# Gated delta-rule scan on one core: the query product of two time steps in one GpSimd instruction

## The reference, cut to what matters

```
def step(state, inp):
    q_t, k_t, v_t, a_t, b_t = inp
    state = a_t[..., None, None] * state
    stored = jnp.einsum('bhij,bhj->bhi', state, k_t)
    delta = b_t[..., None] * (v_t - stored)
    state = state + jnp.einsum('bhi,bhj->bhij', delta, k_t)
    o_t = jnp.einsum('bhij,bhj->bhi', state, q_t)
    return (state, o_t)
_, outs = jax.lax.scan(step, state0, (qT, kT, vT, aT, bT))
```

## Time and profile before

| | us |
|---|---|
| median of 3 runs | 2835.84 |
| lowest, highest | 2834.82, 2837.74 |
| the profiled execution, its own time | 2834.44 |
| its span, first to last instruction | 2832.7 |
| mean granted TensorE clock | 0.788 of full speed |

### The profile page before, as it was taken

The page is one execution under the profiler, slowest core; times in us unless marked ns, Lnnn a source line. Parts: engine busy times, 40 slices in busy tenths (PEclk is TensorE's granted clock), DMA queues, the critical chain, the costliest instruction groups (busy, mean ns, idle before and its releaser), DMA issues. The chain is left out here.

```text
span 2832.7 us, 58672 instructions
## 1 busy us (share of the span) xinstructions
PE 1812.1 (64%) x15340; PEld 1408.9 (50%) x15341; DVE 1967.8 (69%) x5192; ACT 1416.0 (50%) x3723; POOL 1404.3 (50%) x1495
## 2 busy tenths in 40 slices
PE   3666665756454566666338888888886546666661
PEld 2443544435352344545217777777775524454551
DVE  5898888989478544444658888888885694544446
ACT  4666666666322334333217777777776223333331
POOL 2544544445300466666306666666666006666661
PEclk8787776767655788888759999999998557888896
DMA  0000000000240111111521111111111401111116
GB/s 24 12 16 19 23 12 23 13 21 19 72 113 6 32 44 42 43 42 43 151 65 32 34 33 32 35 31 33 33 33 35 105 0 42 43 43 43 43 43 191
DMA packets 184180, 121.31 MB, mean 43 GB/s; under 512 B 23288, under 2 KB 172704, under 8 KB 183968
## 3 DMA queue, kind: packets, MB, share of 16 engines
q1 hardware_dynamic: 146560, 68.36, 9.3%
q0 software_dynamic: 18432, 37.79, 5.0%
q10 hardware_dynamic: 18976, 12.59, 1.5%
HBM read 65.70 MB, written 44.04 MB: 39 GB/s over the span
## 5 line engine op out<-in xcount | busy, mean ns | idle before, releaser
L1735 POOL TENSOR_TENSOR att_pl<-att_p,att_ph 128x384 f16<-128x384 f32 x512 | 461.4, 913 | 280.8 <-ACT att_ph L1951 274.2
L1000 POOL DMA_INDIRECT ffn_xs<-normed,ffn_tokeni x288 | 293.3, 1019 | 415.2 <-DVE ffn_empty L1364 147.8
L324 POOL TENSOR_TENSOR sq<-states,qS 128x256 f32<-128x256 f32 x256 | 241.4, 943 | 355.0 <-DVE states L725 328.2
L537 ACT ACTIVATE decayed<-states,alpha 128x64 f32<-128x64 f32 x1024 | 272.3, 336 | 242.7 <-DVE states L725 241.9
L1006 POOL DMA_INDIRECT picked<-ffn_ys,ffn_targeti x288 | 293.4, 1019 | 185.9 <-DVE ffn_ys L1389 120.9
L1195 ACT ACTIVATE ffn_h<-bank,b_cols 128x256 f32<-128x256 f32 x576 | 234.6, 472 | 277.2 <-PE bank L1097 134.6
L2033 DVE TENSOR_REDUCE att_mx<-bank 128x3 f32<-128x384 f32 x512 | 282.6, 553 | 93.2 <-PE bank L1792 93.2
L1097 PE MATMUL bank<-ffn_xh,w_h 128*128 128x256 f16 x576 | 180.1, 313 | 224.0 <-DVE ffn_xl L1371 144.5
L1948 ACT ACTIVATE att_p<-bank 128x384 f32<-128x384 f32 x512 | 252.4, 493 | 122.2 <-PE bank L1825 115.9
L380 PE MATMUL bank<-sq,ident 128*128 128x128 f32 x1024 | 250.0, 415 | 94.7 <-POOL sq L324 94.7
L380 PEld LDWEIGHTS bank<-sq,ident 128*128 128x128 f32 x1024 | 224.6, 252 | 129.9 <-POOL sq L324 101.7
(11 more groups left out here) (336 smaller groups left out, 5343.0 us busy)
## 6 DMA issues: line engine op xcount, KB each, us to landing
ffn_yg<-picked SPq DMA_DIRECT2D x64, 256.0 KB, 4.7
ffn_x_all<-x SPq DMA_DIRECT2D x16, 512.0 KB, 7.2
normed<-ffn_xn ACTq DMA_DIRECT2D x32, 256.0 KB, 2.3
att_qz<-att_qp SPq DMA_DIRECT2D x256, 32.0 KB, 1.9
ffn_xs<-normed,ffn_tokeni POOLq DMA_INDIRECT x288
picked<-ffn_ys,ffn_targeti POOLq DMA_INDIRECT x288
xin<-in_x SPq DMA_DIRECT2D x64, 64.0 KB, 1.9
xres<-in_x SPq DMA_DIRECT2D x64, 64.0 KB, 2.0
```

What stands on the lines that cost most here:

```text
L324: nc.gpsimd.tensor_tensor(sq[:, t, :].rearrange("p (h i j) -> p h i j", h=HL, i=D), states[:, t, :].rearrange("p (h i j) -> p h i j", h=HL ...
L537: ins = nc.scalar.activation(decayed[:, 64 * h:64 * h + 64], states[:, (t - 1) % TC, 64 * h:64 * h + 64], ACT.Copy, scale=alpha[p][:, t, h ...
L1000: pool.indirect_dma_start(xs[j % AHEAD][:, r, :], None, A["normed"], bass.IndirectOffsetOnAxis(ap=tokeni[:, BR * j + r:BR * j + r + 1], ax ...
L1735: nc.gpsimd.tensor_tensor(pl[:, h % RP, :], p32[:, h % RP, :], ph[:, h % RP, :], ALU.subtract).then_inc(low_done, 1)
```

## The change

POOL issues the product only in odd steps, for that step and the one before it together: 2 x 256 values, with the same waits put together (`state_ready` of the odd step, and at the first pair of a chunk or quarter what the even step waited for), and counts `sq_ready` by two. The side work of POOL keeps its steps; in an even step it now stands behind no product of that step. Nothing else is changed.

```
                 for t in range(TC):
-                    pool.wait_ge(state_ready, c * TC + t + 1)
-                    if t == 0:
-                        pool.wait_ge(prep_dve, prep_at(PREP, c, "q_scan"))
-                    if t % (TC // OQ) == 0 and behind(i, p):
-                        pool.wait_ge(o_sums, OQ * (c - 1) + t // (TC // OQ) + 1)
-                    qb = qS[p][:, 32 * t:32 * t + 32].rearrange("p (h j) -> p h j", h=HL).unsqueeze(2)
-                    nc.gpsimd.tensor_tensor(
-                        sq[:, t, :].rearrange("p (h i j) -> p h i j", h=HL, i=D),
-                        states[:, t, :].rearrange("p (h i j) -> p h i j", h=HL, i=D),
-                        qb.to_broadcast([P, HL, D, D]), ALU.mult).then_inc(sq_ready, 1)
+                    if t % 2 == 1:
+                        a = t - 1
+                        pool.wait_ge(state_ready, c * TC + t + 1)
+                        if a == 0:
+                            pool.wait_ge(prep_dve, prep_at(PREP, c, "q_scan"))
+                        if a % (TC // OQ) == 0 and behind(i, p):
+                            pool.wait_ge(o_sums, OQ * (c - 1) + a // (TC // OQ) + 1)
+                        qb = qS[p][:, 32 * a:32 * a + 64].rearrange("p (th j) -> p th j", j=D).unsqueeze(2)
+                        nc.gpsimd.tensor_tensor(
+                            sq[:, a:a + 2, :].rearrange("p t (h i j) -> p (t h) i j", h=HL, i=D),
+                            states[:, a:a + 2, :].rearrange("p t (h i j) -> p (t h) i j", h=HL, i=D),
+                            qb.to_broadcast([P, 2 * HL, D, D]), ALU.mult).then_inc(sq_ready, 2)
                     if behind(i, p):
```

## The result

| | before | changed |
|---|---|---|
| median, us | 2835.33 (4 runs) | 2861.94 (4 runs) |
| lowest to highest | 2833.94 to 2837.74 | 2854.98 to 2864.99 |
| profiled execution, span | 2832.7 | 2859.8 |

The medians differ by 26.6 us; the ratio is 1.0089 (95% interval 1.007 to 1.0109): slower. The forecast was 2860 in 2843 to 2876.

What follows compares the result with a forecast made beforehand. DVE bounds the scan (busy 614 of 691 us) and POOL idles behind it; 17.9 over 14 chunks, 2.4 at chunk starts, 1.1 in chunk 0, 3.4 in chunk 15 and 0.5 at the end give +25.3, 2860, range 2843 to 2876.

Steps and rivals of the forecast that it cites:

- the gap beneath `delta`: Window of 0.52 us from the end of `prod` to `outer`; a 256-value product just fits, one of 512 doesn't.
- The length of the pair: The 512-value product takes 1.26 us alone, 1.50 beside `prod`, ending 1.55 after `prod`'s start; bounds 1.07 and 1.44.
- Rivals 2 and 3: Rival 2: pair quicker, 1.07, total 2847, chance 0.12. Rival 3: no POOL time saved, pair 1.44, total 2873, chance 0.14.
- step 6: DVE waits 2.1 us for PE there, which covers the pair: 0; the wait at `ab_scan` about unchanged.
- step 12: `log1p` waits for the pair, `beta_v` goes next and `outer` ends later: +0.47 us per chunk.
- steps 10 and 15: Step 10: `h13` and `outer` held, +0.53, `og` ahead of `h11`, +1.01. Step 15: `kabS` before `prod`, -0.88 and +0.78.
- Rival 1: DVE keeps the way while its operations overlap, so steps 10 to 12 get shorter: -6 us, 2828, chance 0.12.
- step 4: 0.7 us of transpose or PSUM work behind `prod` hides the pair: 0.
- Chunk 0: First chunk of the scan, without `ounit` and `og`: about +1.1 us.
- Chunk starts: Pair holds `prod` 0.54 longer, covered by `stats`' wait for the load; `gE` reaches into `outer`: +0.27, 9 times.
- step 2: No side work there; `outer` waits for the pair and ends at 1.84 instead of 1.37: +0.47 us per chunk.

Runs made afterwards that it cites:

- e2: Changed kernel with the even step's product of each pair left out, so half the products are missing: 2709.0 against 2705.97 for the kernel before, ratio 1.0006.
- e3: Kernel before, with only the products of steps 2 and 3 of a chunk made one 512-value operation, beside step 4: 2698.23 against 2705.97, ratio 0.997.
- e1: Changed kernel with POOL also waiting for the state of steps 10 and 14 before their side work: 2713.76 against 2705.97 for the kernel before, ratio 1.0027.

## Why the prediction was right

- *POOL's shorter products give nothing directly.* Right: POOL is busy 57 us less and nothing is faster for it.
- *A POOL operation and a two-input DVE operation exclude each other; the gap beneath `delta` holds 256 values and not 512.* Right, and shown from both sides: half the length at the same place loses nothing (`e2`), the full length beneath a transpose loses nothing (`e3`), and costs 0.47 in the same step of chunk 0, which has no transpose. (`xn`, one tensor and two values per partition, is held too, as the earlier trace rows show.)
- *The length of the pair, 1.26, and 1.55 from `prod`.* The end is 1.55 after `prod` in each of the steps shown. The duration beside `prod`, forecast as 1.50, goes from 1.28 to 1.54 with the moment of issue, 0.27 to 0.01 behind `prod`. Rivals 2 and 3, a quicker and a dearer pair, fall with it. (Rival 2's terms add up to about +0.4 a chunk and not +0.6; nothing hangs on it.) The last pair of the scan, alone:

```profile
754.44 1.26 POOL L326 TENSOR_TENSOR sq<-states,qS 128x512 f32<-128x512 f32 x1 [2.75 <-DVE states L727]
```

- *Steps.* But for step 6 none is off by more than 0.07 us; the largest, step 12, was set too high. The rule that went into steps 10 and 15, that the one issued first goes first, decided +1.01 and held there; `e1` shows the size of it by taking it away. Rival 1, DVE keeping the way wherever its operations overlap, is refuted by step 10: `og`, issued 0.13 before `h11`, goes before it though `outer` still runs. But the observation that the rival started from is there too, in step 4 (last section), so neither rule covers all rows.
- *Chunk 0.* +1.1 forecast, +0.8 measured, and partly luck: the forecast left out step 4, which cost 0.47 there, and step 6 came out 0.64 shorter.
- *Chunk starts.* The sum was near (0.35 for 0.27) and the path to it wrong: I had POOL go first as before, but DVE did, by 0.01 us; the wait for the load then swallowed what `prod` gained. Nor are the nine alike: `prod` waited 0.5 in seven of them before, and `stats` for the load in eight. That the mean came out near is luck.
- *Step 6 as cover.* Right for the pair, but the wait isn't "about unchanged": its row went from 32.0 to 27.9. On the means the steps 6 give back about 2 us, and by so much the scan came out better than the sum. That term I had at zero.
- *Total.* 25.3 forecast for the whole. The median moved by 26.6, of which 23.0 are in the scan and 3.6 outside it, where I had none. The two misses partly cancel, so that the total is nearer than its parts is luck.

The Trainium skill's rule of an exclusive lock ("SBUF — State Buffer", "SBUF: two separate sides") agrees in kind: the later one waits, and the earlier one isn't slowed. Its "for the whole instruction" is a little more than the rows show: in the step 2 above `outer` ends 0.27 behind the pair and not its own 0.42, so up to 0.15 us of the two lie side by side.

## What to carry to other kernels

Fewer and longer operations on an idle engine are no gain by themselves when they and the operations of the engine that bounds the kernel hold each other up: look first at what the bounding engine does in each of its gaps, and give the other an operation that fits the gap. Where a product is taken out of a queue, whatever stood behind it moves up; a wait that pins it to its old place cost nothing here and was worth 19 us. Placed by the gaps, the same work made the kernel 35 us faster, and 45 with the earlier load.

## What the runs showed of the hardware that was not expected

Who goes first is decided by hundredths of a us: at chunk starts `prod` 0.05 behind POOL's product waited 0.5 us, and `prod` 0.01 ahead of the pair made POOL wait instead.

The order of issue isn't the whole rule. In step 4 the product is issued 0.10 before `prod` in the kernel before, the pair 0.03 before it in the changed kernel and in `e3`, and `prod` goes first each time, in all 15 chunks that have an `xn`. In step 10 of the changed kernel `og` is issued 0.13 before `h11` and goes first, in all 14. In both a DVE operation was still running; it was `xn` in the one and `outer`, which POOL had just held, in the other. Which of these differences decides was not tried. The pair of step 4 is free by this order as much as by the transpose: where POOL went first, in step 15 above, `prod` took 1.18.

And the wait of step 6 hangs on TensorE's clock. In chunk 14 the two matmuls for `ab_scan` took 1.91 us in the kernel before and 1.02 in the changed one:

```profile
673.13 1.91 PE L354 MATMUL bank<-xT,wab 128*128 128x512 f32 x2
```

```profile
689.82 1.02 PE L356 MATMUL bank<-xT,wab 128*128 128x512 f32 x2
```

In the kernel before, the granted clock rose from its lower level (1.2 GHz) to the higher (2.4 GHz) right behind these matmuls, in the changed kernel just ahead of them: step 6 of that chunk took 5.30 us and 4.26, within 0.07 in every trace of each. Before the rise PE had summed the last quarter of the chunk before, stood idle for some 4.7 us in both, and begun the new chunk's matmuls. In the changed kernel the quarter's sum began 1.60 after the chunk's start, not 1.06, and the clock had been at the higher level once already, from about the end of that sum into the idle time (0.78 on the mean from 680 to 685; it was 0.50 from 657 to 672 in the kernel before). Which of this is the cause was not tried.
